# Edge search of a graph layer: counting rows and pivots on TensorE in place of pivot gathers, and key blocks gathered in two halves

## The reference

```
src = concat([edge_index[0], loops]); dst = concat([edge_index[1], loops])
e     = leaky_relu(a_src[src] + a_dst[dst], 0.2)
e_max = segment_max(e, dst);   ee = exp(e - e_max[dst])
denom = segment_sum(ee, dst);  alpha = ee / (denom[dst] + 1e-16)
agg   = segment_sum(h[src] * alpha[:, :, None], dst)
```

## Time and profile before

| | us |
|---|---|
| three timed runs: lowest, median, highest | 6648.12, 6649.67, 6666.48 |
| the profiled execution | 6639.78 |
| its span | 6638.1 |

### The profile page before, as it was taken

How to read it: one execution, slowest core, us unless ns; L and a number is a source line. 1 busy time by engine, 2 the same in 40 slices (tenths; PEclk the granted TensorE clock), 3 DMA queues, 4 the chain that set the end, 5 groups by cost and what they waited for, 6 DMA issues and landing times.

```text
span 6638.1 us, 72052 instructions
## 1 busy us (share of the span) xinstructions
PE 2629.1 (40%) x27595; PEld 1957.7 (29%) x28555; DVE 2379.5 (36%) x5304; ACT 1197.0 (18%) x2679; POOL 2645.9 (40%) x2591
## 2 busy tenths in 40 slices
PE   5777777873397844764215454300000000000000
PEld 4666666663232633654113232200000000000000
DVE  7755546666156743771001111311111111101127
ACT  3233323332154422441001110100000000000000
POOL 0000000005300033005755555477777777777560
PEclk8887878885598976985555555555555555555555
DMA  0023222211253000311111111111111111111113
GB/s 27 8 30 43 36 30 34 34 28 11 33 115 68 0 13 12 1 30 26 45 18 41 32 43 28 42 19 19 19 18 18 18 18 14 18 19 18 29 15 108
DMA packets 298413, 196.23 MB, mean 30 GB/s; under 512 B 175469, under 2 KB 262430, under 8 KB 295774
## 3 DMA queue, kind: packets, MB, share of 16 engines
q1 hardware_dynamic: 211230, 150.02, 11.3%
q0 software_dynamic: 82016, 33.49, 5.0%
q10 hardware_dynamic: 4896, 8.92, 0.4%
HBM read 119.54 MB, written 72.71 MB: 29 GB/s over the span
## 4 chain that ended last, share of the span: by engine, by line
PE 27%; POOL 21%; issue 19%; DVE 15%; another core or an unknown queue 13%; ACT 4%; DMA 1%; SPq 0%; ACTq 0%; DVEq 0%; POOLq 0%
PE bank L393 26%; POOL arena L381 21%; DVE arena L1180 1%; DVE arena L1175 1%; DVE arena L935 1%; DVE arena L934 1%; ACT arena L839 1%; DVE arena L940 1%; DVE arena L939 1%; DVE arena L1327 1%; DVE arena L1050 1%; DVE ln_stat L1049 1%; DVE ln_stat L1052 1%; DVE arena L944 0%
## 5 line engine op out<-in xcount | busy, mean ns | idle before, releaser
L393 PE MATMUL bank<-arena 64*64 64x64 f32 (+13 forms) x25478 | 2349.5, 295 | 1325.5 <-ACT arena L839 432.5
L381 POOL DMA_INDIRECT arena<-node_table,arena x2048 | 2119.8, 1035 | 923.4 <-issue 630.9
L393 PEld LDWEIGHTS bank<-arena 64*64 64x64 f32 (+5 forms) x25478 | 1615.9, 166 | 1515.0 <-issue 901.3
L702 PE MATMUL bank<-ident,arena 128*20 128x128 f32 x3 | 0.8, 409 | 1995.2 <-remote 1995.2
L361 POOL MEMSET arena<- 128x512 f32 x1 | 0.5, 530 | 1548.3 <-DVE h_res L1034 1548.3
L702 PEld LDWEIGHTS bank<-ident,arena 128*20 128x20 f32 x3 | 0.3, 111 | 1995.5 <-remote 1995.4
L1225 DVE COPY arena<-arena 128x4 f32<-128x4 f32 x32 | 5.5, 170 | 1318.2 <-DMA arena<-node_table,arena 1317.9
L367 POOL DMA_INDIRECT arena<-sorted_keys,key_block_idx x128 | 120.8, 943 | 698.3 <-DVE key_block_idx L1132 656.6
L1213 DVE TENSOR_TENSOR arena<-bank,arena 128x512 f32<-128x512 f32 x64 | 43.6, 690 | 961.4 <-remote 816.6
L841 ACT ACTIVATE arena<-arena 128x512 f32<-128x512 f32 x32 | 20.1, 629 | 2021.6 <-issue 1303.0
L393 PE MATMUL bank<-ident,arena 128*128 128x128 f32 (+2 forms) x2048 | 285.5, 309 | 236.0 <-ACT arena L810 79.9
(11 more groups left out here) (351 smaller groups left out, 2861.1 us busy)
## 6 DMA issues: line engine op xcount, KB each, us to landing
arena<-expert_gates SPq DMA_DIRECT2D x64, 512.0 KB, 9.2
arena<-node_table,arena POOLq DMA_INDIRECT x2048
sums_sorted<-arena SPq DMA_DIRECT2D x32, 768.0 KB
expert_out<-arena SPq DMA_DIRECT2D x64, 256.0 KB
arena<-expert_out SPq DMA_DIRECT2D x16, 1024.0 KB, 5.5
sort_exchange<-arena SPq DMA_DIRECT2D x14, 1024.0 KB, 4.0
arena<-in_x_dram ACTq DMA_DIRECT2D x34, 256.0 KB, 3.9
edge_dst_terms<-arena SPq DMA_DIRECT2D x1, 4096.0 KB, 21.8
```

Source lines behind the costliest of these rows:

```text
L381: G.indirect_dma_start(out=rch[:,j%NB,c,:],out_offset=None,in_=tbl, in_offset=bass.IndirectOffsetOnAxis(ap=gidx[:,j*CW+c:j*CW+c+1],axis=0) ...
L393: mm=lambda o,a,b,st=True,sp_=True: nc.tensor.matmul(o,a,b,start=st,stop=sp_,skip_group_check=True)
```

## The change

The search becomes two levels, and no pivot is gathered.

- **Rows and pivots by TensorE.** The upper bits of the pivots (the destination, 14 bits) are split into a byte of 6 bits and one of 8 (`pv`). `pvp` is the same, of the row above, fetched by one DMA from partition to partition. `dpv` holds in bf16 a column of ones and the differences of the two bytes between a row and the row above (63 columns in all). `stp` is for 1024 nodes at a time a bf16 matrix of 0 and 1: is the row's first destination at or below the node. A product of `stp` with `dpv` sums the differences over the rows that lie below the node, so it gives the number of such rows and the two bytes of the pivots of the node's own row. VectorE puts the bytes together, compares and sums (`pivots_counted`). There are 16 groups of 8 products, on 8 banks; VectorE builds the matrices two groups ahead.
- **Where.** This stands on VectorE and TensorE between the recurrent block and the first normalisation. The 8 sort steps of L944/L945 in the recurrent block, the broadcast load of the row's firsts, the 128 gathers L364 and the count at iteration 13 are gone.
- **Key blocks in two halves.** POOL gathers 64 (nodes 0 to 8191) once `idx2` is there, and 64 more once `ffn0` has counted the first half (at `k==3`) and has ended on both lanes. Both land in one buffer of 4096 words. The second half is counted at iteration 13 of `attn1`, and `endp` is made at 14.

```diff
-                elif k<=len(NET)+PASS:
-                    t=(k-len(NET)-1)*NT//PASS; n=NT//PASS
-                    dve.wait_ge(s_fr,32)
-                    below(t,n,P,frow[:,:].unsqueeze(1).broadcast_to((P,n,P)),K[1].rearrange("p (t w) -> p t w",w=P),r1)
...
+            for c in range(16):
+                pe.wait_ge(s_sp,c+1)
+                if c>=8: pe.wait_ge(s_sq,c-7)
+                for u in range(8): r=mm(PS[c%8][:,u*64:u*64+63],stp[c%2][:,u*P:(u+1)*P],dpv[:,0:63])
+                r.then_inc(s_sm,1)
...
+            def pivots_counted(c):
+                ts=slice(8*c,8*c+8); v=PS[c%8][:,:].rearrange("p (t k) -> p t k",k=64)
+                dve.wait_ge(s_sm,c+1)
+                lk(V.tensor_scalar(cnt,v[:,:,1:32],256.0,None,ALU.mult))
+                lk(V.tensor_tensor(cnt,cnt,v[:,:,32:63],ALU.add))
+                lk(V.tensor_tensor(cnt,cnt,startp[:,ts].unsqueeze(2).broadcast_to((P,8,31)),ALU.is_lt))
+                lk(V.tensor_reduce(r2[:,ts],cnt,AX.X,ALU.add))
+                V.scalar_tensor_tensor(out=r1[:,ts],in0=v[:,:,0],scalar=32.0,in1=r2[:,ts],op0=ALU.mult,op1=ALU.add).then_inc(s_sq,1)
+            dve.wait_ge(s_ks,32)
+            V.memset(dpv[:,0:1],1.0)
+            for h in range(2): last=V.tensor_tensor(dpv[:,1+31*h:32+31*h],pv[:,h,1:32],pvp[:,h,1:32],ALU.subtract)
+            for c in range(16): last=V.tensor_scalar(fsh[:,c:c+1],first[:,:],-1024.0*c,None,ALU.add)
+            lk(last)
+            dve.wait_ge(s_mc,2)
+            for c in range(16):
+                if c>=2: dve.wait_ge(s_sm,c-1)
+                V.tensor_scalar(stp[c%2],iov,fsh[:,c:c+1],None,ALU.is_ge).then_inc(s_sp,1)
+                if c>=2: pivots_counted(c-2)
+            for c in (14,15): pivots_counted(c)
+            dve.wait_ge(s_sq,16)
+            lk(V.tensor_scalar(r1[:,:],r1[:,:],-32.0,0.0,ALU.add,ALU.max))
+            V.tensor_copy(idx2[:,:],r1[:,:]).then_inc(s_i2,1)
             norm(H[:,:,:],xn)
...
             for k in range(NK):
+                if k==3:
+                    dve.wait_ge(s_l2,16*NT//2)
+                    below(0,NT//2,64,land,land,r3)
+                    V.tensor_copy(rowbase[:,:],rowp_f[:,:]).then_inc(s_i2,1)
...
                 if i==13:
-                    dve.wait_ge(s_l2,16*NT)
-                    below(0,NT,32,land2,land2,r2)
...
+                    dve.wait_ge(s_l3,16*NT//2)
+                    below(NT//2,NT//2,64,land,land,r3)
+                if i==14:
```

More of the change, by code:

```diff
@@ L151, in prog @@
         halves=HALVES
-        s_mc=sem("layer_masks_ready")
+        s_mc=sem("layer_masks_and_node_iota_ready")
         con=bump(D0+4400,S0)
@@ L245, in _ @@
             sp.dma_start(keys2,K[0]).then_inc(s_ks,16)
-            sp.dma_start(piv_d,piv[:,:]).then_inc(s_ks,16)
-            with nc.allow_non_contiguous_dma(reason="one word per row"):
-                sp.dma_start(first_d.unsqueeze(1),piv[:,0:1]).then_inc(s_ks,16)
+            sp.dma_start(pvp[1:P,:,:],pv[0:P-1,:,:]).then_inc(s_ks,16)
             sp.dma_start(ep_d[0:1].unsqueeze(0),zrow[:,:]).then_inc(s_ep,16)
-            sp.wait_ge(s_ks,48)
-            sp.dma_start(frow[:,:],first_d.unsqueeze(0).broadcast_to((P,P))).then_inc(s_fr,16)
+            sp.wait_ge(s_ks,32)
             with nc.allow_non_contiguous_dma(reason="one word per row"):
```

52 lines of the change are left out of this document (26 added, 26 removed).

## The result

The changed kernel takes 6458.7 us (median of four runs, 6444.9 to 6466.6) beside 6648.9 for the kernel before in the same comparison: ratio 0.971, 95% interval 0.968 to 0.973. The forecast was 6468 us, in a range of 6425 to 6540.

A forecast was written before the change was run, and what follows sets the result against it. It took TensorE's stalls beside POOL's gathers in gates and attention, and 2048 later gathers, to bound the kernel. Terms -23+49-68+3-125-18 = -182 us gave execution 6458, or 6468 on the median's side; range 6425 to 6540.

The forecast's parts named there:

- rows out of the recurrent block: Last recurrent iteration loses eight comparisons and eight sums, the one before its exchange steps: -23 us (21 to 27 gained).
- pivot stage: New stage before the first normalisation: VectorE sets the pace at 2.92 us a group, TensorE hidden; +49 us (44 to 62).
- gates' gap: Gates: TensorE loses 88.3 us beside pivot gathers; with 64 gathers starting earlier, 20 remain: -68 us (-88 to -43).
- `ffn0`, group 3: VectorE's 8.9 us of counting the first half is mostly covered by TensorE's lead: +3 us (0 to 9).
- attention's gap: Of 170.4 us lost at iteration 13, 45 remain beside the second 64 gathers at attention's start: -125 us (-140 to -95).
- counts: Attention iterations 13 and 24: less comparing and summing on VectorE, all on the path: -18 us (-17 to -19).
- A: Rival: wider gathers cost more per piece than half, in gates and attention; sum -112, 6538 us; chance 0.15.
- B: Rival: gaps vanish; gates run as if alone, attention loses only until the last gather is issued; 6422 us, chance 0.07.
- C: Rival: gaps in gates and attention come from TensorE's own stream, not the gathers, and remain; +11, 6661 us; chance 0.03.
- D: Rival: the new pivot stage's 128 matmuls meet the slow state, taking 358 us instead of 49; +127, 6777 us; chance 0.03.

The follow-up runs named there:

- the probe: Kernel with second-half gathers six per attention iteration, plus seven stretches of matmuls beside gathers, plain DMAs, fills or nothing behind its end: 7062.1 us.
- the paced stretch: Added stretch behind a kernel's end: matmuls beside 256-byte gathers held to six for each group of matmuls; 84.6 on kind A, against 27.5 us alone.

## Why the prediction was right, point by point

Profile against profile, kind A, in us. "Moved by" is measured at the same point of both traces:

| term | forecast | measured | from |
|---|---|---|---|
| rows out of the recurrent block | -23 | -21.3 | last iteration 88.5 (from 1447.41) for 109.8 |
| pivot stage | +49 | +42.6 | last add to first sum 43.5 for 0.9 |
| gates' gap | -68 | -83.9 | 4.3 left of 88.3 |
| `ffn0`, group 3 | +3 | +6.8 | TensorE's first product to last `back` |
| attention's gap | -125 | -125.1 | 43.6 back beside the second half, 168.7 gone at iteration 13 |
| counts | -18 | -17.5 | the long iteration at 24 |
| drift in attention, mostly the clock | none | +20.3 | see below |
| drift ahead of the last iteration | none | +2.6 | it starts at 1447.41 for 1444.78 |
| span | -182 | -176.2 | 6461.9 for 6638.1 |

The rows add up to -175.5; the other 0.7 lies in the normalisations and behind attention. That the sum came within 6 us of the forecast is in part luck: the gates gave 16 us more than forecast and the pivot stage cost 6 less, while 23 us of drift that no term had went the other way.

**Recurrent block.** Held, within its range. It came out at the low end: 88.5 us is the length of the iteration before it, and no exchange step of that one was worth anything.

**Pivot stage.** The shape held: VectorE sets the pace, TensorE is hidden, and there is no hop between them. The size was 6 us too high, 2.53 us a group for 2.92. Two terms were too dear. The build took 0.74 us, and its successor starts 0.66 after it; I had 0.80 from L989. And of the small steps each comes 0.44 to 0.45 us after the one before (L1064 to L1068), where I had added a read of PSUM at 0.48, and the next build starts 0.08 us after the last of them, where I had 0.17. The Trainium skill ("VectorE: DVE Perf Modes", Mode 2×_2P) gave 0.69 us for the build, and the trace lies between that and my row, nearer to the page's figure in pitch.

**Gates.** The mechanism held: the 64 gathers take 107.3 us from the start of the normalisation (1579.7 to 1687.0), to the microsecond as written. The loss also sets in at the same group as before, the one 105 us behind the start of the normalisation (1683.96). Mis-sized was what follows it: I left 20 us for a long end and a slow restart, and it was 4.3. The last gather was issued at 1687.0 and TensorE was back at 1691.1. My low bound, -88 with nothing left, was the nearer end.

**`ffn0`.** +6.8 lies in 0 to 9. TensorE's lead of two expert pairs covered less of VectorE's 8.9 us than I had taken.

**Attention.** The forecast left 45 us and 43.6 were left. Its working is what the trace shows: the last gather at 2151.2, which is 2203.9 in times of before for the 2201 written, and a start slowed after the first work; only the onset was 6 us and not 12.

**Not forecast: the clock.** Attention's iterations take 17.2 or 18.8 us, and their PT 3.83 or 5.46. In the changed kernel the granted clock is 1.00 (2.4 GHz) over an iteration of the first kind (2200.6 to 2217.8) and 0.90 over one of the second (2252.2 to 2271.0), with 0.69 over its PT, which runs at 1.2 GHz for a part of its time. There 20 of the 32 PT are of the longer kind, and in the kernel before 7: 13 times 1.6 us is the +20. That it belongs to the change no run shows: the kernel before on kind B has eleven of them ahead of iteration 13, the kernel with its gathers under `ffn0` eight in all, and the one that has the cheaper pivot stage besides eighteen.

**The rivals.** A was wrong: block gathers cost no more in the gates than pivot gathers did; the probe even finds 4 and 256 bytes alike. B's two parts split: the gates did run nearly as if alone (4.3 us lost), the attention did not. C is out on kind A by two runs. (The prediction holds against it that no other iteration of attention takes more than 27 us. That was misread: the one at 24 takes 36.4 before, from PT at 2754.64 to 2791.01. It holds VectorE's count, so the argument stands.) The Trainium skill ("SBUF — State Buffer", Who interferes with whom) states that a DMA never contends with a compute engine; the stretches show both sides of it. Plain DMAs beside the matmuls cost nothing (26.9 us for 27.5), as the page has it; gathers through POOL, even of 4 bytes, take the same stream to 98 us on kind A. The page's own exception for descriptors built by GpSimd has GpSimd waiting for VectorE, as its gathers of 4.9 us do here; of TensorE and ScalarE the section says that they never wait on anyone, and if that is meant of more than the memory's ports, the 98 us are against it. D did not come: the pivot stage has no gather beside it, and no slow matmul.

**What I could not have seen.** The forecast's two largest terms, -68 and -125, stand on a behaviour of the chip that was profiled. All rows of before showed it, and nothing in them showed that it is not everywhere. On kind B the offsets of the changed kernel against the one before are -10 us at the last add (the last iteration is 21.5 us shorter and began 11.2 later), +32 at the first sum of the normalisation and at `ffn0`, +39 at attention's start, +9 at its end and +9 in the span; the sum without the gaps is the right one there, and it says "no change".

## What to carry to other kernels

Ask of each gap beside POOL's gathers how many matmuls want to be issued there. Gathers belong beside long matmuls in small bursts (64 in bursts of six under `ffn0`: nothing lost), or in a wait, and not beside a dense stream of short ones, where a microsecond of gathers cost a microsecond of TensorE. Long matmuls alone are no cover: beside an unbroken row of gathers, matmuls of 512 columns too came 2.80 us apart (next section). Before a change is tuned to such a gap, run the kernel unchanged on more than one chip: here the same change was worth 190 us on one kind and nothing on another.

## What the runs showed of the hardware

Two kinds of chip ran the kernel before in 6637 to 6649 and in 5871 to 5876 us. Of the 770 us between the two profiles of before (6638.1 and 5868), 239 are gained by attention's last iteration, where the two gaps lie. The other 531 lie behind it, in the graph layer with its 2048 gathers. The profiles of the changed kernel on both kinds divide them: 54 us in the 128 scatters ahead (220.2 for 166.7), 257 in the first 641 gathers, beside which kind A runs the second expert block, 101 in the 1407 gathers behind it, and 119 behind the last gather. The table of stretches over the second expert block, on kind A and on kind B:

```profile
3022.00:4100.00 1078.00, 462.16 (x1257) 297.17 (x1256) 125.53 (x330) 104.63 (x146) 611.15 (x642) 0.50 0.16 35
2915.00:3557.00 642.00, 431.77 (x1200) 280.56 (x1200) 124.69 (x326) 103.82 (x142) 492.24 (x492) 0.50 0.24 56
```

In the first of them, beside an unbroken row of gathers, TensorE's long matmuls start 2.80 us apart as the short ones do:

```profile
3206.70 1.01 PE L392 MATMUL bank<-arena 64*128 64x512 f32 x1 [2.53 <-issue]
3209.50 1.01 PE L392 MATMUL bank<-arena 64*128 64x512 f32 x1 [1.79 <-issue]
```

So the length of the matmuls is not what spared `ffn0`. The bursts of six may be, or the pace and the clock of its stream (0.98 granted, 0.50 here); no run on kind A tells them apart.

VectorE's stream is hit as well. The pages' groups show its scans behind the table's gathers, with the idle time before them last, on kind A and on kind B:

```profile
L1265 DVE TENSOR_TENSOR_SCAN arena<-arena 128x64 f32<-128x64 f32 x640 | 196.9, 374 | 109.3 <-issue 108.2
L1265 DVE TENSOR_TENSOR_SCAN arena<-arena 128x64 f32<-128x64 f32 x640 | 186.4, 372 | 1.1
```

In the last part of the kernel on kind A, beside the gathers of L388, VectorE's small instructions (0.17 us each) start 1.40 us apart, as at 6189.64 and 6191.03, after idle time that the timeline too puts down to "issue".

At most the first two parts, 311 us, could be had on kind A by keeping POOL's DMAs away from TensorE's work; in the other two TensorE has next to nothing to do. None of this was tried.

What stays open is the inside of the slow stretches. The loss is in the issue of instructions, not in the array: a matmul record is 0.26 us long in them, and the starts lie 2.80 us apart. VectorE's part in the stretch of gathers of one key: the third group of eight matmuls ended at 6533.2, and its fill behind it started at 6586.9, 53.7 us later, where the stretch alone has 0.1. The loss needs an indirect DMA of POOL, is independent of its bytes, begins in the stretches only after 52 to 100 records, and spares `ffn0`, where a matmul comes each 0.24 us and a burst lasts 7.5. Code that is repeated is not spared: in the paced stretch the first turn of the loop, 32 records, took 16.2 us for 3.4. That a supply of fetched instructions runs out would fit the rest; this is argued and no run tested it.
